# Cos and sin products by Strassen's algorithm from the third block on, with norms on ScalarE and pair sums on GpSimd

## The reference

```python
def rfs(xw, ab, AB, gs):                       # xis = ab, AB = exp(xis)
    dot = einsum('...d,rd->...r', xw, ab[:, None] * gs)
    corr = (0.5 * sum(xw * xw, -1))[..., None] * (ab * ab)
    return 1 / sqrt(512) * AB * exp(dot - corr)
x = L0_attn_x                                  # (4, 2048, 512) f32
a = einsum('bsr,or->bso', rfs(x, ...), rfs(input_weights, ...))
x = layernorm(x + a)
real = einsum('bti,io->bto', x, cos(theta + theta_noise))
imag = einsum('bti,io->bto', x, sin(phi + phi_noise))
out = layernorm(x + sqrt(real * real + imag * imag))
```

## Time and profile before

| what | value |
|---|---|
| median of 3 runs | 764.31 us (764.07 to 764.36) |
| profiled execution | 763.54 us |
| its span | 761.7 us |
| granted TensorE clock, mean | 0.994 |
| TensorE busy | 746.9 us, 98% |
| VectorE busy | 492.5 us, 65% |
| ScalarE busy | 373.6 us, 49% |
| GpSimd busy | 169.8 us, 22% |

### The profile page before, as it was taken

The page is one execution under the profiler, slowest core; times in us unless marked ns, Lnnn a source line. Parts: engine busy times, 40 slices in busy tenths (PEclk is TensorE's granted clock), DMA queues, the critical chain, the costliest instruction groups (busy, mean ns, idle before and its releaser), DMA issues.

```text
span 761.7 us, 10414 instructions
## 1 busy us (share of the span) xinstructions
PE 746.9 (98%) x3396; PEld 615.7 (81%) x3396; DVE 492.5 (65%) x891; ACT 373.6 (49%) x643; POOL 169.8 (22%) x306
## 2 busy tenths in 40 slices
PE   9999899999999999999999999999999999999995
PEld 7878778888888888888888888888888888888884
DVE  5897865747476584756747575574847747475464
ACT  6837555362635636264462625636264453725322
POOL 5862202213031120301212030120302112030222
PEclk9999999999999999999999999999999999999998
DMA  9850131404113040321405013140311405010001
GB/s 288 233 158 0 56 125 42 138 0 140 39 55 124 28 151 0 89 90 41 138 0 171 8 57 123 28 151 0 114 65 41 138 18 161 0 69 0 28 28 56
DMA packets 32750, 60.75 MB, mean 80 GB/s; under 512 B 3168, under 2 KB 3168, under 8 KB 32736
## 3 DMA queue, kind: packets, MB, share of 16 engines
q1 hardware_dynamic: 31584, 58.50, 23.4%
q0 software_dynamic: 1152, 2.10, 1.7%
HBM read 43.78 MB, written 16.81 MB: 80 GB/s over the span
## 4 chain that ended last, share of the span: by engine, by line
PE 90%; DVE 5%; ACT 2%; issue 1%; DMA 1%; SPq 0%; POOL 0%; POOLq 0%; DVEq 0%; ACTq 0%
PE token_ps L504 14%; PE token_ps L506 14%; PE token_ps L505 14%; PE token_ps L556 7%; PE token_ps L555 7%; PE token_ps L554 7%; PE project_ps L493 7%; PE project_ps L495 7%; PE project_ps L494 7%; PE turn_ps L562 3%; DVE stats L740 1%; DVE cos_lo L650 1%; PE turn_ps L513 0%; PE token_ps L520 0%; PE token_ps L523 0%
## 5 line engine op out<-in xcount | busy, mean ns | idle before, releaser
L294 POOL TENSOR_TENSOR var_eps<-mv,eps 128x1 f32<-128x1 f32 x128 | 41.0, 320 | 566.7 <-DVE mv L744 566.5
L405 ACT ACTIVATE late<-token_ps 128x512 f32<-128x512 f32 x120 | 71.7, 599 | 131.5 <-PE token_ps L506 131.5
L397 ACT ACTIVATE zT_hi<-turn_ps 128x512 fp32r<-128x512 f32 x64 | 38.2, 598 | 175.0 <-PE turn_ps L562 174.9
L493 PE MATMUL project_ps<-xT_hi,gs_hi 128*128 128x512 f32 x248 | 101.7, 410 | 1.0 <-DVE expo L655 1.0
L650 DVE TENSOR_TENSOR xT_lo<-xT_raw,xT_hi 128x512 fp32r<-128x512 f32 x64 | 44.5, 704 | 85.9 <-ACT xT_hi L445 85.5
L554 PE MATMUL token_ps<-W_hi,F_hi 128*128 128x512 f32 x256 | 99.7, 389 | 0.0
L556 PE MATMUL token_ps<-W_hi,F_lo 128*128 128x512 f32 x256 | 99.6, 389 | 0.0
L555 PE MATMUL token_ps<-W_lo,F_hi 128*128 128x512 f32 x256 | 99.6, 389 | 0.0
L495 PE MATMUL project_ps<-xT_hi,gs_lo 128*128 128x512 f32 x248 | 98.0, 395 | 0.0
L755 DVE TENSOR_TENSOR late<-z,late 128x512 f32<-128x512 f32 x64 | 44.3, 692 | 82.4 <-ACT late L439 81.8
L494 PE MATMUL project_ps<-xT_lo,gs_hi 128*128 128x512 f32 x248 | 97.4, 393 | 0.0
(11 more groups left out here) (126 smaller groups left out, 1315.9 us busy)
## 6 DMA issues: line engine op xcount, KB each, us to landing
xT_raw<-in_xT SPq DMA_DIRECT2D x16, 1024.0 KB, 6.1
x_tok<-in_x SPq DMA_DIRECT2D x16, 1024.0 KB, 7.0
out_tokens<-o_tile SPq DMA_DIRECT2D x64, 256.0 KB, 2.0
norm_bc<-token_norms SPq DMA_DIRECT2D x15, 256.0 KB, 3.5
trig<-in_gsT SPq DMA_DIRECT2D x4, 256.0 KB, 5.0
z<-in_wT SPq DMA_DIRECT2D x4, 256.0 KB, 5.2
trig<-in_theta SPq DMA_DIRECT2D x4, 256.0 KB, 5.8
trig<-in_theta_noise POOLq DMA_DIRECT2D x4, 256.0 KB, 7.6
```

What stands on the lines that cost most here:

```text
L405: nc.scalar.activation(dst, bank[:, :], ACT.Square).then_inc(square_done, 1)
L493: nc.tensor.matmul(o, gs_hi[:, c, cols], rhs_hi[:, c, :], start=(c == 0), stop=False)
```

## The change

Blocks 0 and 1 stay as they are in what they compute. From block 2 on the two products of a block with cos and sin are taken as one product of 2x2 blocks, [A11 A12; A21 A22], the two halves of z's columns for a pair of token tiles (row 1 is tile 2p, row 2 tile 2p+1), times [cos upper, sin upper; cos lower, sin lower]. By Strassen's algorithm in Winograd's form it takes 7 products of half the depth (two chunks, 6 matmuls) in place of 8: M1 = A11 B11, M2 = A12 B21, M3 = S4 B22, M4 = A22 T4, M5 = S1 T1, M6 = S2 T2, M7 = S3 T3. The four sums T of the right side are made once, in block 1. The four half sums S (128x256 each) are made by VectorE for each pair, rounded by ScalarE as one 128x1024 operation and split by VectorE as another. Seven joins on VectorE (U = M1 + M6 and so on) turn the products into the four results; M1 is first copied to SBUF by ScalarE.

```diff
+        PLAIN = 2
+        QUARTER_ORDER = ["M1", "M6", "M7", "M5", "M2", "M4", "M3"]
+        QUARTER_ORDER_LAST = ["M1", "M4", "M2", "M6", "M7", "M5", "M3"]
...
+            def turn(b, j):
+                pe.wait_ge(z_made, C * b + j + 1)
+                if j >= 2:
+                    pe.wait_ge(half_sums_made, 8 * (b - PLAIN) + 4)
+                transposes(j)
...
+            def quarter_product(o, left, right):
+                for i in range(H):
+                    nc.tensor.matmul(o, left[0][i], right[0][i], start=(i == 0), stop=False)
+                    nc.tensor.matmul(o, left[0][i], right[1][i], start=False, stop=False)
+                    last = nc.tensor.matmul(o, left[1][i], right[0][i], start=False, stop=(i == H - 1))
+                last.then_inc(quarter_done, 1)
...
+                    for j in range(C):
+                        mix(b, j)
+                    pe.wait_ge(xT_lo_made, C * (b + 2))
+                    if not behind_plain:
+                        pe.wait_ge(joined, joins_ahead + 7)
+                    for j in range(C):
+                        pe.wait_ge(expo_made, C * (b + 2) + j - 1)
+                        project(j, project_ps[j % 2])
+                        if j < 2:
+                            turn(b, j)
+                    turn(b, 2)
+                    turn(b, 3)
+                    pair_products(b, 0, more)
...
+                pair_products(b, 1, more)
```

```diff
+            def pair_sum(b, p):
+                pool.wait_ge(square_done, 2 * C * b + C * p + C + SQUARE_CREDIT)
+                pool.tensor_tensor(parts[:, p, :, 0, :], parts[:, p, :, 0, :], parts[:, p, :, 1, :], ALU.add).then_inc(sum_made, 2)
...
+            def step(b, last=False):
+                pair_sum(b - 1, 1)
+                scale1(b, 0)
+                pair_residual2(b - 1, 1)
+                scale1(b, 1)
+                if not last:
+                    pair_scale2(b - 1, 1)
+                scale1(b, 2)
+                scale1(b, 3)
+                if last:
+                    pair_scale2(b - 1, 1)
+                pair_sum(b, 0)
+                pair_residual2(b, 0)
+                pair_scale2(b, 0)
```

On ScalarE both norms are an Identity with scale and bias, and squares, roots and the rounding of x's columns are 128x1024:

```diff
+                if more:
+                    pair_roots(b - 1, 1)
+                    norm1(0)
+                    norm1(1)
+                    norm2(b - 1, 2)
+                    norm2(b - 1, 3)
+                    norm1(2)
+                    norm1(3)
+                    round_first(0)
+                    features(C * (b + 2), 0, 0)
+                    round_second(0)
+                    features(C * (b + 2) + 1, 1, 1)
+                    round_half_sums(0)
+                    features(C * (b + 2) + 2, 2, 0)
+                    round_first(1)
+                    round_second(1)
+                    features(C * (b + 2) + 3, 3, 1)
...
+                square_tile(0, 1)
+                square_tile(0, 0)
+                if ahead:
+                    round_columns(1)
+                copy_first(1)
+                pair_roots(b, 0)
+                if ahead:
+                    act.wait_ge(x_loaded[slot], 16 * (pair + 2))
+                    for j in range(C):
+                        sum_square(b + 3, j, slot, 1 - slot)
+                norm2(b, 0)
+                norm2(b, 1)
+                square_tile(1, 1)
+                square_tile(1, 0)
```

On VectorE, the front and the tail of a block:

```diff
+                residual1(b, slot, 1)
+                moments1(0)
+                stats1(b, 1)
+                if more:
+                    stats1_made(b, 1)
+                    pair_stats2(b - 1, 1, 0)
+                    moments1(1)
+                    pair_stats2(b - 1, 1, 1)
+                    pair_stats2_made(b - 1, 1)
+                    residual1(b, slot, 2)
...
+                    split_first(0)
+                    next_exponent(b, slot, 1)
+                    split_second(0)
+                    half_sums(0)
+                    split_feature_pair(C * (b + 2) + 1, 0)
+                    next_exponent(b, slot, 2)
+                    split_half_sums(0)
+                    next_exponent(b, slot, 3)
+                    split_first(1)
+                    split_second(1)
+                    half_sums(1)
+                    join_u(0)
+                    join_v(0)
+                    join_c22(0)
+                    join_w(0)
+                    split_half_sums(1)
+                    join_c11(0)
+                    split_feature_pair(C * (b + 2) + 3, 1)
+                    join_c21(0)
...
+                join_c12(0)
+                if ahead:
+                    split_columns(b + 2, 0)
+                join_u(1)
+                if ahead:
+                    split_columns(b + 2, 1)
+                join_v(1)
+                join_c22(1)
+                join_w(1)
+                if ahead:
+                    turn_norms(b + 3, 1 - slot)
+                pair_stats2(b, 0, 0)
+                join_c11(1)
+                pair_stats2(b, 0, 1)
+                pair_stats2_made(b, 0)
+                join_c21(1)
+                pair_moments2(0)
+                join_c12(1)
```

More of the change, by code:

```diff
@@ L317, in _ @@
+            with pool.Fori(PLAIN, NB - 1) as b:
                 step(b)
-            last_inverse_root2(NB - 1)
+            step(NB - 1, last=True)
+            root2(NB - 1, 2, tile=3)
+            root2(NB - 1, 3, tile=2)
         @block.scalar
@@ new lines, in mix_part, with mix @@
+            def mix_part(j, c):
+                cols = slice(j * P, (j + 1) * P)
+                o = token_ps[j][:, :]
+                nc.tensor.matmul(o, F_hi[:, c, cols], W_hi[:, c, :], start=(c == 0), stop=False)
+                nc.tensor.matmul(o, F_hi[:, c, cols], W_lo[:, c, :], start=False, stop=False)
+                return nc.tensor.matmul(o, F_lo[:, c, cols], W_hi[:, c, :], start=False, stop=(c == C - 1))
+            def mix(b, j):
+                for c in range(C):
+                    last = mix_part(j, c)
+                last.then_inc(mix_done, 1)
@@ L619, in step @@
+            def step(b, more, behind_plain=False):
+                pe.wait_ge(F_made, C * (b + 1))
+                joins_ahead = 2 * JOINS * (b - PLAIN) - JOINS + JOIN_CREDIT
+                if behind_plain:
+                    pe.wait_ge(square_done, 2 * C * b + SQUARE_CREDIT)
+                else:
+                    pe.wait_ge(joined, joins_ahead + 5)
                 if more:
+                    for j in range(C):
+                        mix(b, j)
                     pe.wait_ge(xT_lo_made, C * (b + 2))
+                    if not behind_plain:
+                        pe.wait_ge(joined, joins_ahead + 7)
@@ L801, in step @@
+                    stats1(b, j)
                     if j >= 1:
[L802 to L810 removed]
```

1036 lines of the change are left out of this document (682 added, 354 removed).

## The result

The changed kernel takes 848.72 us (median of 4 runs, 846.11 to 851.71) beside 764.34 for the kernel before on the same chip: a ratio of 1.1106, 95% interval 1.1086 to 1.1126. The forecast was 825 us, in a range of 790 to 850, so the direction was right, the time lies just inside the upper end, and 24 us of the loss were missed. The profiled execution has a span of 843.9 us, 82.2 more than before.

What follows compares the result with a forecast made beforehand. It took a circle of waits through ScalarE, GpSimd and VectorE as the bound, 48.9 us a block: 763.5 + 5.3 (block 1) + 1.4 (block 2) + 42 (twelve blocks) + 15 (last) = 827, taken as 825 us, range 790 to 850.

Steps and rivals of the forecast that it cites:

- a circle of waits: Per block, waits through ScalarE, GpSimd and VectorE close in 48.9 us, 3.5 more than before, without TensorE's pace; chance 0.76.
- Step (a): Tail of the block before: statistics, joins, pair scale to Y + 4.2, output tiles, second pair's squares to Y + 7.4.
- Y: The moment ScalarE has finished the four sums of squares of the block before; the next first mix starts at Y + 1.45.
- t: Time in us within a block, counted from its first mix matmul on TensorE, which starts at Y + 1.45.
- Steps (b) to (e): GpSimd's sum, scale, residual to 12.2; VectorE onwards, half sums 25.3; products and joins, C12 38.3; squares to sums of squares, 47.5.
- the loss of block 2: Block 2 finds block 1's last square early, so GpSimd's turn ends 2.1 us sooner: 46.8 us, a loss of 1.4.
- Block 1's term of 5.3: Block 1 makes, rounds and splits four wide sums; its last square, behind two output tiles, ends at 50: +5.3 us.
- The last block's 15: Block 15, 43.0 us before, becomes 58: late joins to 46.6, last squares to 50.7, then 7.3 us: +15.
- TensorE was no bound (730): Rival: TensorE stays the bound and the removed matmuls pay, 730 us, if the circle is under 42.7; chance 0.10.
- both faster cases: TensorE bound at 730 us, chance 0.10; wide GpSimd sum at a narrow one's 1.3 us, 765 us, chance 0.06.
- Contention: Rival: every GpSimd pair sum takes 3.2 us, adding 3 us a block, 861 us in all; chance 0.08.
- up to 4 us a block: By the skill's rule, GpSimd's four sums on the circle take 9.8 us where VectorE would spend under 5.

Runs made afterwards that it cites:

- kernel 3: Changed kernel with one matmul of three left out of the mix from block 1 on (output less exact): 846.31 us.
- kernel 4: Changed kernel plus 12 dummy matmuls of 128x512 into a free bank before each mix, from block 3 on: 846.93 us.
- kernel 1: Changed kernel with ScalarE's squares of the second pair issued ahead of the two output tiles: 835.21 us.
- kernel 2: Changed kernel with VectorE's three last joins issued ahead of the statistics and the transposition that wait for GpSimd: 828.95 us.
- kernel 6: Changed kernel with VectorE's joins first, ScalarE's squares ahead of output tiles, and GpSimd's second residual ahead of tile 0's scale; engines unchanged: 782.62 us.
- kernel 12: Changed kernel with ScalarE's second-pair squares ahead of the output tiles and 8 dummy matmuls before each mix: 811.46 us.
- kernel 10: Changed kernel with only block 2's start altered: the mix no longer waits for the split quarter sums, which are rounded and split earlier: 839.24 us.
- kernel 7: kernel 6 with the wide sums and residuals on VectorE as well, placed as in kernel 9: 770.10 us.
- kernel 8: kernel 7 with block 2's start and the last block reordered, including the first pair's second residual ahead of the second pair's joins: 751.02 us.
- kernel 5: Changed kernel with the sums of squares and residuals of blocks 2 to 15 moved from GpSimd to VectorE, order around them kept: 853.21 us.
- kernel 9: kernel 5 with the second pair's sum one tile earlier on VectorE and its residual ahead of one aggregate: 818.66 us.

## Why the prediction was right, and where it was short

*What bounds it.* Right: a circle of waits, and not TensorE. Busy shares alone (no engine above 88%) would have said that there is room; the walk from queue to queue said 48.9 us a block, and 49.86 came. Kernels 3 and 4 show that TensorE's pace is not in it, kernels 1, 2 and 6 that the order is: the same instructions take 44.8 or 49.9 us. That the time fell inside the range is partly luck. Every term of the sum that was clearly off was too small, and 848.7 is above the circle's own 800 to 848 and 1.3 us below the end of the wider range.

*Step (a).* The first mix at Y + 1.45: measured Y + 1.47. Then it slips. The pair's scale was to end at Y + 4.2 and ended at 337.60, Y + 4.6; the two output tiles took 1.43 in place of 1.26, with the norm mis-sized. The squares ended at 341.14, t = 6.65 in place of 5.95. These 0.7 us a block, the scale's own start and power (0.71 for two columns, 0.55 for one) and the price of a norm, are most of the missing 1.0.

*Steps (b) to (e).* The wide sum 2.40 (2.45), tile scale 1.24 (1.25), residual's end t = 12.87 (12.2), half sums' end 26.15 (25.3), C12 at 39.0 (38.3), Y again at 48.4 (47.45): nearly the same lag all along, 0.2 us more at the end. TensorE waited for the half sums 0.7 us in place of 2.6, since it came to turn 2 late: 1.7 us from the mix, and 0.6 idle before the last projection (an exponent, L984) with the slower start behind it.

*What it did not see.* After 2.7 us idle the mix of nine of the twelve blocks runs in part at the lower clock. In the block shown the prediction had mix results at 2.9 and 5.6 us and they came at 4.6 and 7.3. In the circle it had no price, by 1.0 us of slack (kernel 4), but it made a shorter circle longer (kernels 1 and 12). It also fits the loss of block 2, where GpSimd waited 6.5 us for the moments of tile 0: 3.8 us in place of 1.4, and 1.6 in kernel 10, where the clock stays full.

*The ends.* Block 1's term of 5.3 came as 7.6. The prediction put the last square last; in fact TensorE waited for the split of the fourth quarter sum (L979), behind a rounding that stood behind the same two output tiles, 6.4 us. The last block's 15 came as 17.8, and 2 us had been taken off the sum besides. So the sum is short by 11 in the twelve blocks, 5 in the first three, 3 in the last and these 2; the other 3 us are the median's distance from the profiled execution, the shortest of the four at 846.11.

*The rivals.* TensorE was no bound (730), and a wide sum costs as two narrow ones (2.42 against 1.28), so both faster cases fell. Contention is small in the changed kernel: GpSimd's wide sums are 2.38 to 2.42 nearly everywhere, VectorE's split at 327.33 takes 1.47 in place of 1.22 beside one of them, 0.25 us on a queue that waited anyway. With the exclusive lock of the rule weighed there (the Trainium skill, SBUF — State Buffer, SBUF: two separate sides) the trace agrees. In kernels 7 and 8, where the circle is short, the same contention reaches the path and costs 0.8 us in every second block. (The operation at 54.08 is a split, high part from raw, and not a residual; the argument needs only its two inputs in SBUF.)

*The rule on elementwise work.* The Trainium skill (GPSIMD Engine Reference, Engine selection) has GpSimd at about half of VectorE's speed with two inputs; 2.40 against 1.22 agrees. But the gain of "up to 4 us a block" needed the right places: as a bare move it gained nothing (kernel 5, blocks 0.4 us longer, and 0.1 to 0.4 shorter where few matmuls were slow), moved by one tile it gave 2.1 (kernel 9), and in the reordered kernel 1.0 (7 against 6).

## What to carry to other kernels

When a bound engine is relieved, write out the next block leg by leg along the queues, and sum the circle; busy shares say nothing of it. Of an in-order queue ask what stands behind the waiting instruction: moving three kinds of instruction by a place or two was worth more (5 us a block) than halving the price of four (2.1 at most). And an edit that gains nothing alone may gain much beside another, since slack in one leg hides it: test pairs when single edits fall short of their sum.

## What the runs showed of the hardware that was not expected

An idle stretch of 2.7 us on TensorE can be enough to lower the clock: matmuls at 335.08 and 335.51 stand 0.43 us apart against 0.227 at full clock, the granted clock over 5.0 us is 0.66, between the two levels of 1.2 and 2.4 GHz, and full speed is back some 3.5 us after the start. In kernel 2 1.8 us idle, before a projection, was enough in six of twelve blocks. With dummy matmuls in the gap, which leave no idle stretch over 1.2 us there, it stays full in all twelve (kernels 4 and 12). It is not so in every block: with the same 2.7 us idle, blocks 5, 10, 13 and, after 2.51 us, 15 of the changed kernel are at full speed throughout, and others start fast and slow down 0.3 to 1.3 us later. What decides it was not settled.

A two-column operation of GpSimd can take 1.08 us in place of 0.19 when it starts beside a wide VectorE operation with both inputs in SBUF, and ends with that operation (kernel 8, 352.96). So moving wide work from GpSimd to VectorE did not end the contention between the two; it moved it to GpSimd's small operations, which here stand on the path.
